# A two-layer kernel with Mamba, attention and expert FFNs: loads and weights in another order, ScalarE writing layer 1's normalised rows, and parts of the last attention turns moved

## The reference

```python
x = L0_attn_u                                  # 16 sequences x 256 tokens x 256
xn = _layernorm(x)
x = x + mamba(xn, ...) + moe_ffn_0(xn, ...)    # 8 experts, top 2, inner size 512, and a shared FFN
xn = _layernorm(x)
x = x + attention(xn, w_qkv, w_o) + moe_ffn_1(xn, ...)  # 16 heads of 16, causal; 8 experts, top 2, inner 128, shared 256

def _layernorm(x, axis=-1, eps=1e-05):
    m = jnp.mean(x, axis=axis, keepdims=True)
    v = jnp.var(x, axis=axis, keepdims=True)
    return (x - m) / jnp.sqrt(v + eps)
# an expert FFN: y = sum over the token's top-2 experts of cw[t,e] * (silu(x @ wg[e]) * (x @ wu[e])) @ wd[e]
# attention: softmax(q k^T / 4, causal) v, then @ w_o, for each sequence
```

## Time and profile before

| | before |
|---|---|
| median of 3 runs | 1408.76 us (1407.96 to 1412.47) |
| the profiled execution, its time | 1414.86 us |
| its span, first to last instruction | 1413.0 us |
| granted TensorE clock, mean | 0.985 |
| TensorE busy | 1318.1 us (93%), 10668 instructions |
| VectorE busy | 911.1 us (64%) |
| GpSimd busy | 653.3 us (46%) |
| ScalarE busy | 511.3 us (36%) |
| DMA mean over the span | 72 GB/s |

### The profile page before, as it was taken

The page is one execution under the profiler, slowest core; times in us unless marked ns, Lnnn a source line. Parts: engine busy times, 40 slices in busy tenths (PEclk is TensorE's granted clock), DMA queues, the critical chain, the costliest instruction groups (busy, mean ns, idle before and its releaser), DMA issues.

```text
span 1413.0 us, 30111 instructions
## 1 busy us (share of the span) xinstructions
PE 1318.1 (93%) x10668; PEld 1039.2 (74%) x10684; DVE 911.1 (64%) x3115; ACT 511.3 (36%) x1096; POOL 653.3 (46%) x801
## 2 busy tenths in 40 slices
PE   7899999999999999899999889999998978999985
PEld 6788889888888888766766556666665647888874
DVE  4566534555556655499998788888888753333356
ACT  2122122222222222333333355565565634444431
POOL 2356423333333332455554144545544454677772
PEclk9999999999999999999999899999999999999998
DMA  9922951111111114600000111010110001233376
GB/s 340 222 43 31 75 100 59 46 46 46 51 48 46 46 49 158 187 1 0 0 0 0 53 39 47 24 47 24 47 46 9 10 2 54 94 103 102 129 228 233
DMA packets 77446, 102.05 MB, mean 72 GB/s; under 512 B 13021, under 2 KB 65260, under 8 KB 77312
## 3 DMA queue, kind: packets, MB, share of 16 engines
q1 hardware_dynamic: 59200, 62.35, 17.0%
q0 software_dynamic: 18112, 37.93, 8.3%
HBM read 64.26 MB, written 35.98 MB: 71 GB/s over the span
## 4 chain that ended last, share of the span: by engine, by line
PE 73%; DVE 11%; issue 7%; POOL 6%; DMA 1%; ACT 1%; another core or an unknown queue 0%; SPq 0%; DVEq 0%; POOLq 0%
PE score L1891 42%; PE mixed L1891 16%; PE side L1891 9%; DVE score L1729 4%; POOL y_rows L847 2%; PE side L2135 2%; POOL sh_dn L839 1%; PE side L1901 1%; POOL XN L839 1%; DVE ARENA L1737 1%; PE mixed L2345 1%; DVE WGU L1729 1%; POOL ARENA L812 1%; DVE X L1848 1%; POOL lists L777 1%
## 5 line engine op out<-in xcount | busy, mean ns | idle before, releaser
L839 POOL DMA_INDIRECT XN<-xn_rows,slot_tok x106 | 108.2, 1021 | 217.8 <-PE side L2135 191.3
L1729 DVE CUSTOM_DVE_ANT_0 score<-score,future_b 128x128 f32<-128x128 f32 (+1 forms) x512 | 167.3, 389 | 42.1 <-PE score L1891 41.5
L847 POOL DMA_INDIRECT y_rows<-sh_gu,slot_row x144 | 144.4, 1003 | 89.5 <-ACT sh_gu L1040 50.6
L875 POOL TENSOR_SCALAR_AFFINE_SELECT ARENA<-ARENA 128x256 f32<-128x256 f32 x256 | 102.7, 424 | 158.3 <-ACT ARENA L1080 158.1
L1891 PE MATMUL score<-xT,HT 128*128 128x128 f32 x912 | 167.2, 275 | 0.0
L1080 ACT ACTIVATE ARENA<-score 128x768 f32<-128x768 f32 x128 | 103.9, 811 | 136.8 <-PE score L1891 136.5
L1891 PE MATMUL score<-ARENA 32*128 32x256 f32 (+1 forms) x2048 | 127.3, 354 | 25.6 <-DVE WGU L1729 14.6
L777 POOL DMA_INDIRECT lists<-token_no,w_in x128 | 125.3, 979 | 34.5 <-issue 30.2
L1891 PEld LDWEIGHTS score<-xT,HT 128*128 128x128 f32 x912 | 134.0, 192 | 0.0
L812 POOL TENSOR_TENSOR ARENA<-tri_le,DT 128x1024 bf16<-128x1024 bf16 x48 | 90.2, 1894 | 88.8 <-PE mixed L1891 35.7
L1040 ACT ACTIVATE sh_gu<-mixed 128x256 f32<-128x256 f32 x144 | 55.2, 383 | 207.9 <-PE mixed L1891 207.9
(11 more groups left out here) (309 smaller groups left out, 2810.8 us busy)
## 6 DMA issues: line engine op xcount, KB each, us to landing
WGU<-in_gu SPq DMA_DIRECT2D x8, 1024.0 KB, 14.8
WGU<-y_rows SPq DMA_DIRECT2D x32, 256.0 KB, 3.1
ARENA<-y_rows SPq DMA_DIRECT2D x32, 256.0 KB, 3.9
xn_rows<-XN SPq DMA_DIRECT2D x24, 256.0 KB
X<-in_u SPq DMA_DIRECT2D x16, 256.0 KB, 8.5
ARENA<-in_dn SPq DMA_DIRECT2D x8, 512.0 KB
x_parked<-X SPq DMA_DIRECT2D x4, 1024.0 KB
X<-x_parked SPq DMA_DIRECT2D x4, 1024.0 KB
```

The lines of the kernel that those rows point to most:

```text
L839: x["got"][j % ring].mark(eng.indirect_dma_start(XG[j % ring], None, xn_rows[l], bass.IndirectOffsetOnAxis(slot_tok[:, col:col + 1], 0)))
L847: x["out"][j % YRING[l]].mark(eng.indirect_dma_start(y_rows[g], bass.IndirectOffsetOnAxis(slot_row[:, col:col + 1], 0), yo(l, j), None))
L875: ins = eng.affine_select(out=m, in_=m, compare_op=ALU.is_ge, fill=0.0, base=0, pattern=[[0, 2], [1, P]], channel_multiplier=-1)
L1729: ins = eng.tensor_tensor_reduce(s, s, future, -1.0, BIG, ALU.add, ALU.min, NM[:, c, j, at:at + 1])
```

## The change

The diff has these parts.

- SyncE: the x loads go one per turn of the loop, always six sequences ahead, and the down weights go one per turn of the loop from n=1 to n=7.
- Layer 1's norm apply moves from VectorE to ScalarE for sequences 1 to 15 (sequence 0 stays on VectorE): an activation Identity with scale rstd and bias centre = −mean·rstd. GpSimd makes centre with two more operations and a wait.
- `turn_maxima(b, 0)` stands behind `scores(0, now(2), ...)` when there is no d.
- The last pair's second pick and the rank matmuls move; `table_index(2)` goes from turn 17 to turn 18; `ffn_up(1, of(0))` with its silu goes from turn 19 to turn 18, in two parts around `weigh(3)`; its product stays in turn 19.
- A constant minus_one, tile_e in the place of list_f, shared semaphore names, statistics waiting for the apply two sequences back.

```diff
@@ SyncE @@
-            for ahead in range(n + (6 if n < 2 else 8), min(n + (7 if n < 1 else 9), NSEQ)):
-                load_x(ahead)
+            if n + 6 < NSEQ:
+                load_x(n + 6)
             N[0]["xn"].wait(eng, n)
...
             if n == 1:
                 eng.wait_ge(s_zero, 32)
-                for e in range(E - 1):
-                    load_down(e)
+            if 0 < n < E:
+                load_down(n - 1)
@@ GpSimd, norm_stage @@
+            if l == 1 and r.n:
+                eng.tensor_tensor(centre[r.u][:, :], mv[r.u][:, :, 0], minus_one[:, :], ALU.mult).then_inc(s_centre, 1)
+                eng.tensor_tensor(rstd[r.u][:, :], rstd[r.u][:, :], minus_half[:, :], ALU.pow).then_inc(s_centre, 1)
+                eng.wait_ge(s_centre, 2 * r.n)
+                ne["rstd"].mark(eng.tensor_tensor(centre[r.u][:, :], centre[r.u][:, :], rstd[r.u][:, :], ALU.mult))
+                return
@@ ScalarE @@
+        def norm_apply(r):
+            ne = N[1]
+            ne["rstd"].wait(eng, r.n)
+            ne["stored"][r.u].wait(eng, r.half, 1)
+            ne["tr"].wait(eng, r.n, 2)
+            for c in range(CH):
+                ins = act(XN[r.u][:, c, :], X[:, r.n * CH + c, :], ACT.Identity, bias=centre[r.u][:, c:c + 1], scale=rstd[r.u][:, c:c + 1])
+            ne["xn"].mark(ins)
...
-            if o and not d:
-                ffn_silu(1, of(0))
...
+            if d and not b:
+                ffn_silu(1, of(0), True, [0])
             if d:
                 mixed_copy(d, 1)
+            if d and not b:
+                ffn_silu(1, of(0), True, [1])
...
             if a:
                 k_copies(a, 1)
+            if c and c.n:
+                norm_apply(c)
@@ VectorE, attention @@
             if d:
                 shift(d, 1)
-            if a and b and b.v == 1:
+            if b and b.v == 1:
                 pick_experts(1, b.i, [1])
+            if d and not b:
+                table_index(2)
...
-            if b and not a:
-                table_index(2)
...
-            if c:
-                norm_apply(1, c)
...
-            if a and a.n == NSEQ - 1:
-                pick_experts(1, a.i, [1])
@@ TensorE, attention @@
-            if b and not a:
-                A["qc"].wait(eng, 2 * b.n + 1)
-                rank_tokens(1, NSEQ // 2 - 1)
-            elif b:
+            if b and a:
                 values(b, 0)
...
             scores(1, now(0), held(2))
-            if o and not d:
-                eng.wait_ge(s_l1b, 16 * (3 + 2 * E + 1))
-                ffn_up(1, of(0))
             if o:
                 turn_out(o, d)
+            if b and not a:
+                A["qc"].wait(eng, 2 * b.n + 1)
+                rank_tokens(1, NSEQ // 2 - 1)
...
-            if b:
-                if d:
-                    A["oc"].wait(eng, 2 * d.n)
+            if b and d:
+                A["oc"].wait(eng, 2 * d.n)
                 turn_maxima(b, 0)
             scores(0, now(2), held(3))
+            if b and not d:
+                turn_maxima(b, 0)
...
+            if d and not b:
+                eng.wait_ge(s_l1b, 16 * (3 + 2 * E + 1))
+                A["exp"][0].wait(eng, NSEQ * GROUPS - 1)
+                ffn_up(1, of(0), "last turn", [0])
             if d:
                 weigh(d, 3)
...
+            if d and not b:
+                ffn_up(1, of(0), "last turn", [1])
```

More of the change, by code:

```diff
@@ L263, in program @@
     minus_half = sb("minus_half", [P, CH])
+    minus_one = sb("minus_one", [P, CH])
     iota_e = iota_j[:, 0:E]
@@ L310, in program @@
     rstd = [sb(f"rstd{u}", [P, CH]) for u in range(2)]
+    centre = [sb(f"centre{u}", [P, CH]) for u in range(2)]
     LG = sb("LG", [P, NT, E])
@@ L324, in program @@
     ex_i = sb("route_experts_i", [P, 2, E], I32)
-    tile_e = sb("tile_e", [P, WHOLE_COLS + BLOCK_COLS])
     row_no = sb("row_no", [P, 2])
@@ L347, in program @@
     list_f, list_i = ra.take(P), ra.take(P).bitcast(I32)
+    tile_e = list_f
     tile_cmp = Area(w_out[:, :, :].rearrange("p k n -> p (k n)")).take(KD * D // (E - 1), E - 1)
@@ L435, in program @@
     UP_PARTS = [(0, 0, I0 // P, HTt[1][:, :, P:2 * P]), (1, 0, I0 // P, spare)]
-    s_const, CONSTS = sem("const"), 20
+    s_const, CONSTS = sem("const"), 21
     XL = [ev(f"load_x{part}", 0, 16) for part in range(4)]
@@ L453, in norm_events @@
         return n
-    norm_chain = sem("norm_chain")
+    norm_chain, s_centre = sem("norm_chain"), sem("norm_centre")
     N = [norm_events(0), norm_events(1)]
@@ L539, in program @@
     A["rchain"] = Chain(pair_chain, 1, NSEQ)
-    A["y"] = [[ev(f"a_y{u}{k}", 0, 16) for k in range(TOPK)] for u in range(2)]
+    A["y"] = [[ev(f"rows_loaded{TOPK * u + k}", 0, 16) for k in range(TOPK)] for u in range(2)]
     s_fill = sem("attention_fill")
     s_hmask = sem("head_mask")
-    FY = [ev(f"fin_y{u}", 0, 16) for u in range(4)]
+    FY = [ev(f"rows_loaded{u}", 0, 16, None, NSEQ // 2) for u in range(4)]
     FO = [ev(f"fin_out{k}", 1, 16, "sync") for k in range(2)]
@@ L735, in _ @@
         for t, v in ((ident, 0.0), (tri_le, 1.0), (tri_gt, 1.0), (quarter_le, 0.25),
-                     (ones_b, 1.0), (before_b, 1.0), (future_b, 0.0), (minus_half, -0.5)):
+                     (ones_b, 1.0), (before_b, 1.0), (future_b, 0.0), (minus_half, -0.5), (minus_one, -1.0)):
             eng.memset(t[:, :], v).then_inc(s_const, 1)
@@ L932, in pair_copy, with ffn_silu @@
                 logits_copy(0, a.i)
-        def ffn_silu(l, r, late=False):
+        def ffn_silu(l, r, late=False, parts=None):
             f, ni = FF[l], FF[l]["ni"]
-            for i in range(ni):
+            for i in parts or range(ni):
                 n = r.n * ni + i
@@ L1718, in stats_stage @@
             A["comb"].wait(eng, r.n)
+            N[1]["xn"].wait(eng, r.n, 2)
             norm_stats(1, r)
@@ L1777, in attention @@
                 maxima(b, 1, 1)
-            if b and not a:
-                table_index(2)
             if o and not d:
                 for i in range(FF[1]["ni"]):
-                    gate_product(1, of(0), i)
+                    gate_product(1, of(0), i, True)
                 add_down(1, of(0))
@@ L1944, in turn_list, with ffn_up @@
             ins.then_inc(s_turned, 1)
-        def ffn_up(l, r, late=None):
+        def ffn_up(l, r, late=None, parts=None):
             f, ni = FF[l], FF[l]["ni"]
```

## The result

The changed kernel takes 1403.06 us (median of 20 runs, 1398.04 to 1418.73); the kernel before took 1408.78 us over as many. The ratio is 0.9958, interval [0.9941, 0.9976]: 5.9 us faster, between 3.4 and 8.3. The forecast was 1395 with a range of 1389 to 1403.5. The direction was right; the gain is 44% to 65% of the 13.5 us forecast. In two later sessions every kernel, before too, took 1463 to 1511 us, in a slower state of the chip; their times decide little.

A forecast was written before the change was run, and what follows sets the result against it. TensorE, busy 1318.1 of 1413.0 us (93%), was taken as the bound; only its idle and low-clock time could be won. Gains of 5.5 + 3.4 + 0 + 4.6 = 13.5 us off 1408.76 gave 1395, range 1389 to 1403.5.

The forecast's parts named there:

- Loads and stores of layer 0: TensorE's 3.95 us gap at 59.84 us goes with an earlier store of sequence 2, plus 1.5 us low clock: 5.5 us.
- the step that took the upper end: Layer 0's loads and stores: 5.5 us taken from 0 to 5.5, since 9.8 us is more than the 8.86 needed.
- a later down load: Layer 0: a later down load may hold up a later store, one reason for the lower end of 0.
- the memset and the table's new place: Constant minus_one's memset among GpSimd's constants and the table's new place in memory: said to cost nothing.
- Maxima of the first full turn: A score pass moves into TensorE's 2.76 us idle before VectorE's turned maxima: 3.4 us, between 1.65 and 5.4.
- of the 9.13 us from there to 807.47 the 1.65 us pass is already done: First full turn, from 798.3 us: the pass moved into the gap saves its 1.65 us, the lower end.
- The second half: First full turn: a shortened gap keeps TensorE's clock up; 1.75 us taken, about half of a possible 3.74.
- Steady turns: ScalarE's apply and GpSimd's bias in 22.3 us turns: 0 forecast, bounds +1.5 and −2 us.
- The rival of the shared port: Steady turns: GpSimd's new operations clash with VectorE's, costing 8.4 us; part of "nothing moves", 1404 to 1413, chance 0.10.
- End of attention: Last turns: moved picks, rank matmuls, table_index and ffn_up gain 4.6 us, bounds 1 and 6 us.
- The pieces: End of attention: rank matmuls 1.33, GpSimd's earlier selections 2.98, ffn_up filling waits 1.14 and 0.49, minus 1.3 us.
- the exposed normalise: End of attention, last sequence: normalise and turn_out lose the cover of ffn_up's 16 matmuls, costing some 1.3 us.

The follow-up runs named there:

- only_apply: Kernel before with only layer 1's norm apply on ScalarE and centre on GpSimd, plus needed names and tensors, minus_one ahead of X; ratio 1.0050 [1.0029, 1.0070].
- after: The changed kernel with the whole diff, first session, against the kernel before; 1403.06 us, ratio 0.9958 [0.9941, 0.9976].
- after_d: The changed kernel timed again in another session, against the kernel before; median 1405.1 us over 12 runs, ratio 0.9938 [0.9909, 0.9966].
- only_loads: Kernel before with only SyncE's new order of loads, down weights and stores; ratio 0.9968 [0.9945, 0.9991].
- apply_aligned_b: Kernel before with the apply on ScalarE alone and minus_one behind the small tensors, X at its old address; second timing, ratio 1.0010 [0.9990, 1.0030].
- shift_32_b: Kernel before with an unused tensor moving X and all behind it 32 bytes, tile_e in list_f's place; second timing, ratio 1.0045 [1.0025, 1.0065].
- shift_64: As shift_32_b with two unused tensors, everything from X on 64 bytes further than in the kernel before; ratio 1.0033 [1.0013, 1.0054].

## Why the prediction was right or wrong

**Loads and stores of layer 0: right in its place, given back in part.** Forecast 5.5 us. S12 to S30 is 56.7 us on the mean of seven traces with the old order (55.9 without only_apply's 61.7) and 50.7 on the mean of five with the new: 5.2 to 6.0 us. The mechanism stands: the store of sequence 2 was late, and now that it is issued earlier the gap is gone. What failed is the step that took the upper end and set nothing against it. The prediction named a later down load as a reason for the lower end and gave it no price. In the changed kernel's own trace TensorE is held up at 91.76, and from the start to Y0 it gains 1.9 us on before; over after and after_d it is 2.1 us on the mean, against the four old-order traces named under the sum. The hold-up lies where the spread loads share the DMA engines with GpSimd's scatters (0.80 of the time busy from 80 to 90 us, 0.21 before), but only_loads has 1.12 there and no hold-up, so that this is the cause is argued and not shown. Part is chance: in after_d the stretch up to S12 is 1.7 us longer than in before because sh_gu, issued at 3.18 us ahead of everything that changed, kept TensorE waiting for 2.28 us and not 0.81.

**A term put at nothing: the place of minus_one.** The prediction says that the memset and the table's new place cost nothing, and doesn't ask what the constant moves. It moves X and all behind it by 32 bytes, which takes 2 to 3% of the rate of the weight loads and, in the kernel before, 5 to 6 us. In the changed kernel its price is open, as said above.

**Maxima of the first full turn: the wrong step.** Forecast 3.4 us, measured 0 to 0.7. The step "of the 9.13 us from there to 807.47 the 1.65 us pass is already done" took the pass for work that TensorE had to wait to do. VectorE is the limit of that turn (in the changed kernel it idles for 0.59 us in all from 788.7 to 797.5): the pass moved into the gap, and the next pass then waits 1.02 us for VectorE's next maxima, with 1.26 still ahead of the turned ones. 0.59 + 1.26 + 1.02 = 2.87 us for 2.76. The second half, 1.75 us for a clock that stays up, failed too: it falls in every trace, and where the edit shortens its stay at half, from 10.2 to 6.8 us, that is worth 0.7 us. The 0 is the difference of the means, 88.4 us on both sides.

**Steady turns: right.** Forecast 0, measured 0.2 us in ten turns (C16 to C176). The pair took 1.08 us where 1.02 was taken; the exponential behind it starts at once. The Trainium skill (VectorE: DVE Perf Modes, The TRN2 errata) would make a pair from SBUF 1.11 us, an estimate, and the trace agrees. The rival of the shared port fell: GpSimd's new operations take 0.2 us each, and ten turns together are longer by 0.2 us at most. The exclusive lock of the Trainium skill (SBUF — State Buffer, Who interferes with whom) isn't refuted by this: VectorE's L1378 took 0.89 us beside GpSimd's selection of 1153.88 in the last turn, where the same operation took 0.16 before, off the path.

**End of attention: right, the sum somewhat small.** Forecast 4.6, measured 6.0 on the means and 4.3 between the profiles of before and after (84.0 to 79.7). The pieces came out: GpSimd's idle of 2.98 us closed, and TensorE's 3.68 us are 0.76, 2.92 less; the exposed normalise cost 1.18 us for 1.3; table_index takes 4.1 us for 3.2 in its new place, hidden. Two pieces were left out of the sum: 0.71 us that TensorE waited at 1170.36 for ScalarE's copy (sh_gu), gone now, and 0.73 us of the slow pass at 1148.59. The changed kernel pays some back: its clock is at half for 3.4 us from 1130 us on too, so that a score pass and a weigh take 1.67 and 1.51 us for 0.94 and 0.86.

**The sum.** The means of the stretches give 6.0 + 0 + 6.0 − 0.2 = 11.8 us. The profiles of the changed kernel (1404.2 and 1404.5) lie 8.8 us under the mean of 1413.1 of four traces without the three gains (before, apply_aligned_b, shift_32_b, shift_64). Stretch by stretch against these four, layer 0 up to Y0 gives 2.1 us, C208 to S66 4.8, and all the rest 1.8, for which there was no term. The ratios say 5.9 [3.4, 8.3] and 8.8 [4.8, 12.9] us. So the 13.5 us were too many by nearly the whole 3.4 us for the maxima and by 3.4 of the 5.5 us in layer 0; the other stretches give 2 us back. That the first session measured 3 us less than the second lies within the two intervals.

**What stays open.** The shift of 32 or 64 bytes costs the kernel before 5 to 6 us in the ratios, and its profiled spans (1414.4 and 1412.6 us, for 1412.6 in apply_aligned_b) show hardly any of it. only_apply's trace has 6 us at the gap of 60 us. That the late store is what passes the lower rate on to TensorE isn't shown: the two shifts have a gap of the old size. What stops TensorE within matmuls that wait for nothing at 91 us isn't settled either. A rival that no run tests is that the engine waited for its own program, which is loaded by DMA too; against it, the trace has no packet of its two instruction queues from 80 to 96 us, so none is seen that could have ended the stops.

## What to carry to other kernels

A gap that one engine leaves isn't time to be won until the next wait of the same engine is written down: fill it with work that feeds the same late engine, and the wait returns behind the work. When a large transfer is spread out, its load moves into a later stretch, and that stretch has to be priced too. Where the granted clock of two traces differs ahead of an edit, as here at 766 us, compare only traces that agree there before the edit is called worth something or nothing. Small constants belong behind the large buffers in the order of allocation: look at the byte address of each transfer's destination before and after an edit.

## What the runs showed of the hardware that was not expected

Transfers into SBUF buffers at a multiple of 256 bytes of the partition ran at 417 to 420 GB/s in the window of 20 to 30 us (eleven traces), at 407 to 410 with everything moved by 32, 64 or 128 bytes (nine traces), and at 418 again by 256. A packet of 4096 bytes took 159 to 160 ns against 163 to 164.
